# Four batches across the partitions in the gradient memory of a decoder block

## The reference, cut to what matters

```
k, v, q = causal_dwconv(hidden @ W.T)        # 32 features each, four taps
alpha, eta, theta = mean over 32 features of sigmoid / sigmoid / softplus gates
for c0 in range(0, S, CHUNK):                # 4 chunks, each needs the state of the one before
    g = grad of sum((silu(k_t @ W1.T) @ W2.T - v_t)**2), state of the chunk's start
    g = g * min(1 / norm(g), 1)              # per token
    Sm = eta*Sm - theta*g;  Wm = (1-alpha)*Wm + Sm      # a scan over the 64 tokens
    h = silu(q_t @ W1t);  out_t = h @ W2t    # with the state of each token
out = rmsnorm(retrieved @ Wo.T) * (hidden @ gW.T + gb); x = layernorm(x + out)
```

## Time and profile before

| | us |
|---|---|
| median of 3 runs (lowest, highest) | 4791.35 (4788.69, 4794.55) |
| profiled execution, its own time | 4782.92 |
| its span, first to last instruction | 4780.8 |
| `memory_inputs`, first matmul to the next block's first | 12.68 to 86.04 |
| the four `memory_chunk` blocks, to the last copy's end | 86.04 to 218.72 |
| `memory_output`, to its last copy's end | 219.69 to 256.74 |

### The profile page before, as it was taken

One profiled execution on the slowest core, in us unless ns is written; L12 is line 12 of the kernel. 1 busy time (PEld: TensorE's weight loads), 2 busy tenths in 40 slices (PEclk: granted clock), 3 DMA queues, 4 the chain that ended last, 5 costly groups with the idle time before them and its releaser, 6 DMA issues. The chain is left out here.

```text
span 4780.8 us, 75879 instructions
## 1 busy us (share of the span) xinstructions
PE 3821.7 (80%) x28979; PEld 2194.7 (46%) x28979; DVE 3405.9 (71%) x5269; ACT 2397.6 (50%) x3237; POOL 1424.3 (30%) x1078
## 2 busy tenths in 40 slices
PE   5740887999999999999983748849985858888873
PEld 3630445666666666666652424424433422222222
DVE  5478665778777877878784247667755658888868
ACT  2120224666666666666661125526662437776772
POOL 0000432666666666666673340000000000000000
PEclk6565898999999999999996769969996869999996
DMA  0010840000000000000002163145521342332300
GB/s 20 1 55 0 182 129 28 1 15 15 1 15 1 15 1 15 1 15 1 1 1 89 54 165 50 24 81 83 84 36 34 83 83 46 51 47 49 51 2 9
DMA packets 155463, 194.79 MB, mean 41 GB/s; under 512 B 23685, under 2 KB 117502, under 8 KB 154468
## 3 DMA queue, kind: packets, MB, share of 16 engines
q1 hardware_dynamic: 144068, 167.17, 17.5%
q0 software_dynamic: 9856, 22.67, 1.8%
q10 hardware_dynamic: 1184, 0.12, 0.0%
HBM read 145.03 MB, written 42.42 MB: 39 GB/s over the span
## 5 line engine op out<-in xcount | busy, mean ns | idle before, releaser
L3127 POOL TENSOR_TENSOR arena<-arena 128x512 f32<-128x512 f32 (+1 forms) x768 | 1133.0, 1477 | 630.1 <-ACT arena L3081 575.9
L2574 ACT ACTIVATE arena<-ps 128x1024 f32<-128x1024 f32 (+1 forms) x688 | 703.1, 1023 | 329.4 <-PE ps L2499 319.0
L2592 DVE TENSOR_REDUCE arena<-ps 128x2 f32<-128x826 f32 (+1 forms) x576 | 564.9, 981 | 183.4 <-PE ps L2445 175.1
L3143 DVE TENSOR_TENSOR arena<-arena 128x1024 f32<-128x1024 f32 (+1 forms) x448 | 653.1, 1497 | 34.9 <-ACT arena L3110 34.9
L3165 DVE TENSOR_TENSOR arena<-ps,arena 128x512 f32<-128x512 f32 (+1 forms) x768 | 530.3, 691 | 109.1 <-ACT arena L3075 75.6
L2445 PE MATMUL ps<-arena 48*128 48x413 bf16 (+3 forms) x1920 | 436.5, 334 | 132.2 <-DVE arena L2592 64.3
L3075 ACT ACTIVATE arena<-ps 128x1024 f32<-128x1024 f32 (+1 forms) x448 | 410.4, 960 | 200.6 <-PE ps L3003 194.2
L3081 ACT ACTIVATE arena<-arena 128x1024 f32<-128x1024 f32 (+1 forms) x448 | 425.0, 992 | 60.4 <-DVE arena L3143 57.9
L2518 PE MATMUL ps<-arena 128*9 128x256 f32 (+2 forms) x5504 | 436.1, 389 | 10.2 <-ACT arena L2562 7.4
L3003 PE MATMUL ps<-arena 64*128 64x256 f32 (+1 forms) x3328 | 427.4, 391 | 5.8 <-ACT arena L3097 1.3
L3017 PE MATMUL ps<-arena 128*64 128x256 f32 (+1 forms) x3328 | 411.1, 387 | 6.5 <-ACT arena L3081 6.5
(11 more groups left out here) (661 smaller groups left out, 5341.3 us busy)
## 6 DMA issues: line engine op xcount, KB each, us to landing
arena<-ctx_parts SPq DMA_DIRECT2D x96, 200.1 KB
arena<-ctx_parts SPq DMA_DIRECT2D x192, 100.1 KB
arena<-fs_rows SPq DMA_DIRECT2D x128, 128.0 KB, 7.2
arena<-in_ctx_feat SPq DMA_DIRECT2D x8, 1601.0 KB, 6.4
arena<-in_ctx SPq DMA_DIRECT2D x16, 768.0 KB
arena<-diff_att_stack SPq DMA_DIRECT2D x60, 192.0 KB, 6.6
ctx_parts<-arena SPq DMA_DIRECT2D x24, 400.2 KB, 7.7
arena<-in_ctx_feat SPq DMA_DIRECT2D x8, 800.5 KB, 9.4
```

Source lines behind the costliest of these rows:

```text
L2574: act.activation(self.prob[0:rows, u % 3, :], self.ps[0:rows, 2 * (u % 2):2 * (u % 2) + 2, :].rearrange("p n c -> p (n c)"), ACT.Exp).then ...
L2592: ins = dve.tensor_reduce(dst[:, :, j // 2], self.ps[:, 4:6, 0:hi - lo], AX.X, ALU.max)
L3127: pool.tensor_tensor(acc[0:rows, u % 2, :], before, sc[0:rows, u % 2, t, :], ALU.add).then_inc(added, 1)
L3143: dve.tensor_tensor(e, e, mb[0:rows, u % 2, None, :].to_broadcast([rows, n, 2 * S]), ALU.subtract).then_inc(sub_done, 1)
```

## The change

The eight batches become four groups q of two batches j. The four groups go across the partitions (32 features each, 128 in all) and the two batches stay in the columns. Column counts per instruction fall to a quarter: 512 in `memory_inputs`, 128 in a chunk. The states become block-diagonal 128x128 matrices (`state`, `W2`, `kM`, `h0M`, `GM`, `GM2`, `woM`, with zeros that POOL writes once), so that one matmul serves four batches. Where a product must stay 32 wide (projections, the clipped products `inside`, the updates), four matmuls write four different 32-partition groups of PSUM.

```diff
+            def project(bank, name, g):
+                for q in range(NQ):
+                    ins = pe.matmul(ps[rows_of(q), bank, :], W(name)[:, g * HM:(g + 1) * HM],
+                                    x_feat[:, q * BANK:(q + 1) * BANK], start=True, stop=True)
+                ins.then_inc(s["proj_ready"], 1)
...
-                ins = pe.matmul(ps[0:96, 4 + n, :], W("wgate"), x_feat[:, n * BANK:(n + 1) * BANK],
+            project(BANK_OF_GATE[ALPHA], "wgate", ALPHA)
+            project(BANK_OF_GATE[ETA], "wgate", ETA)
+            project(BANK_OF_PROJ[KEY], "wkvq", KEY)
+            project(BANK_OF_GATE[THETA], "wgate", THETA)
+            project(BANK_OF_PROJ[QUERY], "wkvq", QUERY)
+            project(BANK_OF_PROJ[VALUE], "wkvq", VALUE)
+
+            for n, g in enumerate((ALPHA, ETA)):
+                pe.wait_ge(s["sig_ready"], n + 1)
+                pe.matmul(ps[:, 6 + n, :], W("same"), gates[:, g, :], start=True,
+                          stop=True).then_inc(s["rates_f"], 1)
...
+            by_token(0, ALPHA)
...
+            by_token(2, ETA)
```

```diff
...
+            for c in range(NCH + 1):
+                if c:
+                    e = c - 1
+                    if e:
+                        pe.wait_ge(s["out_copied"], e)
+                    open_bank()
+                    carried(e, 0, feat["qA"][:, :, e, :], feat["qB"][:, :, e, :])
+                    pe.wait_ge(s["gm_ready"], c)
+                    pe.wait_ge(s["cg_ready"], c)
+                    inside(e, 1, GM).then_inc(s["y_ready"], 1)
+                if c < NCH:
+                    if c:
+                        pe.wait_ge(s["w1_ready"], c)
+                    for j in range(NJ):
+                        ins = pe.matmul(two(z)[:, j, :], state[:, c % 2, 0, 0, j, :], key[:, j, c, :], start=True, stop=True)
+                    ins.then_inc(s["z_ready"], 1)
+                    for q in range(NQ):
+                        ins = pe.matmul(ps[:, KQ, q * P:(q + 1) * P], kM[:, q, c * P:(c + 1) * P], query[:, :, c, :],
+                                        start=True, stop=True)
+                    ins.then_inc(s["kq_ready"], 1)
...
+                    for j in range(NJ):
+                        ins = pe.matmul(two(pred)[:, j, :], state[:, c % 2, 0, 1, j, :], two(h0[c % 2])[:, j, :],
+                                        start=True, stop=True)
+                    ins.then_inc(s["pred_ready"], 1)
+                    pe.transpose(turned_h, h0[c % 2], ident[:, :]).then_inc(s["turned_h"], 1)
+                if c:
+                    pe.wait_ge(s["h_ready"], c)
+                    pe.wait_ge(s["h0M_ready"], c)
+                    for q in range(NQ):
+                        ins = pe.matmul(ps[:, HH, q * P:(q + 1) * P], h0M[:, e % 2, q, :], h, start=True, stop=True)
+                    ins.then_inc(s["hh_ready"], 1)
...
+                    for j in range(NJ):
+                        ins = pe.matmul(two(pred)[:, j, :], W2[:, j, :], two(dp)[:, j, :], start=True, stop=True)
+                    ins.then_inc(s["dh_ready"], 1)
+                    pe.transpose(turned[:, 0:P], dp, ident[:, :])
...
+                if c:
+                    pe.wait_ge(s["hab_ready"], c)
+                    open_bank()
+                    carried(e, 1, two(hA), two(hB))
...
+                if c:
+                    pe.wait_ge(s["gm2_ready"], c)
+                    inside(e, 0, GM2).then_inc(s["out_ready"], 1)
+                if c < NCH - 1:
+                    pe.wait_ge(s["cgw1_ready"], c + 1)
+                    for j in range(NJ):
+                        for q in range(NQ):
+                            ins = pe.matmul(two(got[0])[rows_of(q), j, :], ktok[:, c, j, rows_of(q)], cgw[1][:, q, :, :],
+                                            start=True, stop=True)
+                    ins.then_inc(s["upd0_ready"], 1)
...
```

```diff
+                if 0 < c < NCH:
+                    dve.wait_ge(s["upd0_ready"], c)
+                    ins, src0 = renew(c, 0)
+                    ins.then_inc(s["w1_ready"], 1)
...
+                    link(ins)
+                    dve.transpose(W2[:, :, :], state[:, c % 2, 0, 1, :, :]).then_inc(s["w2_ready"], 1)
...
+                    dve.wait_ge(s["dh_ready"], c + 1)
+                    link(tt(da, pred, silu, ALU.mult))
+                    dve.sem_inc(s["da_ready"], 1)
...
+                    dve.wait_ge(s["norm_a_ready"], c + 1)
+                    at = slice(c * NQ, (c + 1) * NQ)
+                    link(tt(n2, norm_a, m["knorm"][:, at], ALU.mult))
+                    tt(n2, n2, np_h, ALU.add).then_inc(s["norm_ready"], 1)
+                    dve.wait_ge(s["root_ready"], c + 1)
...
+                        link(tt(coef_w[:, :, :], m["ends"][:, c, :, :], coef[:, :, None].to_broadcast([P, NQ, 2]), ALU.mult))
+                        for n, ready in ((1, "cgw1_ready"), (0, "cgw0_ready")):
+                            src = by_q(turned[:, n * P:(n + 1) * P])[:, :, None, :].to_broadcast([P, NQ, 2, HM])
+                            tt(cgw[n][:, :, :, :], src, coef_w[:, :, :, None].to_broadcast([P, NQ, 2, HM]),
+                               ALU.mult).then_inc(s[ready], 1)
```

```diff
-                ins = pe.matmul(out[:, t, :], m["ret"][:, t * P:(t + 1) * P], W("woT"), start=True, stop=True)
+            for n in range(4):
+                ins = pe.matmul(ps[:, n, :], m["ret"][:, n * P:(n + 1) * P], m["woM"][:, :, :], start=True, stop=True)
```

More of the change, by code:

```diff
@@ L391, in memory_inputs @@
         st = Stage(env, ctx, "mem_in")
[L392 to L399, removed]
@@ L422, in _ @@
[L422 to L431, removed]
@@ L440, in _ @@
+            pe.wait_ge(s["theta_in"], 1)
+            for c in range(NCH):
+                ins = pe.matmul(ps[:, 6, c * NQ:(c + 1) * NQ], theta[:, c * P:(c + 1) * P], means[:, :, 0],
+                                start=True, stop=True)
+            ins.then_inc(s["sums_ready"], 1)
         @block.scalar
         def _(act):
-            link = Chain(act, act_own)
-            act.wait_ge(gate_in, 1)
-            act.activation(gates[0:64, :], ps[0:64, 4:8, :], ACT.Sigmoid, bias=W("gate_b")[0:64, :]).then_inc(sig_ready, 1)
@@ new lines, in _ @@
+            act.wait_ge(s["kturn_ready"], 1)
+            for j in range(NJ):
+                copy(m["ktok"][half(j), :, j, :], ps[half(j), 7, :].rearrange("p (c f) -> p c f", f=P))
+        @block.gpsimd
+        def _(pool):
+            pool.memset(first[:, :, :], 0.0).then_inc(s["firsts_ready"], 1)
+            for name in ("state", "now", "W2", "kM", "ktok", "woM"):
+                ins = pool.memset(m[name], 0.0)
+            ins.then_inc(s["zeros_ready"], 1)
+            for name in ("h0M", "GM", "GM2", "htok", "zero"):
+                pool.memset(m[name], 0.0)
+            pool.wait_ge(s["soft_ready"], 1)
+            pool.tensor_tensor(chunk_first(theta), by_chunk(gates[:, THETA, :]), by_chunk(soft[0]),
+                               ALU.add).then_inc(s["theta_in"], 1)
@@ L466, in _ @@
[L466 to L482, removed]
@@ new lines, in open_bank, with carried, inside @@
+            def open_bank():
+                pe.matmul(yo, m["zero"][:, 0:P], m["zero"][:, P:2 * P], start=True, stop=False)
+            def carried(c, n, a, b):
+                for j in range(NJ):
+                    pe.matmul(two(yo)[:, j, :], state[:, c % 2, 0, n, j, :], a[:, j, :], start=False, stop=False)
+                    pe.matmul(two(yo)[:, j, :], state[:, c % 2, 1, n, j, :], b[:, j, :], start=False, stop=False)
+            def inside(c, n, g):
+                for q in range(NQ):
+                    ins = pe.matmul(yo[rows_of(q), :], cg[c % 2][:, n, q, :], g[:, q, :], start=False, stop=True)
+                return ins
```

537 lines of the change are left out of this document (298 added, 239 removed).

## The result

The changed kernel takes 4652.63 us (median of 4 runs, 4646.32 to 4663.57), the kernel before 4790.02 in the same rounds (4780.89 to 4794.55). The ratio is 0.9726, with an interval of 0.9706 to 0.9746: faster. Forecast: 4670, 121.4 us less. Measured: 137.4 less, then 119.8.

The account below looks back on a forecast made before the run. DVE was taken to set memory_inputs' end, one PE-ACT-DVE chain the chunks. Gains 42.7 (memory_inputs) + 78.0 (chunks) + 3.5 (memory_output) - 2.8 (array shapes) = 121.4, from 4782.92 to 4661.5, as median 4670; range 4651 to 4698.

Parts of the forecast that it names:

- Projections: In memory_inputs: 12 fourfold passes, 5.8 us, plus 1.5 for a start at half clock, 7.3 in all.
- DVE's list in `memory_inputs`: From the rates on, DVE sets the end of memory_inputs: its steps together 20.4 us.
- Weight slab: 27% larger, it lands under the turning of x before 12.68; without that cover it would cost 1.9 us.
- Rounds: Chunks: a round takes 16.0 us at half clock, 11.2 at full; clock rises and falls, so the middle, 13.6.
- Rival (2): Chunks: clock rises in the second round and stays, chunks 48 us, memory_output 2 less; total 4661; chance 0.15.
- Array shapes (0.1 each): Changes between column groups and full width cost 0.1 us, about seven a round, 2.8 over the program.
- The table loads that I counted as hidden: Chunks: both ACT table loads lie between other steps and cost nothing; uncovered, each would cost 1.3 us a round.
- (1): Clock stays at half in chunks and projections: rounds 16.0, last 21.9, projections and sums 4.8 more; 4683; chance 0.20.
- (3): 32-wide matmuls of projections, clipped groups and updates do not overlap: 34 us more, 4704; chance 0.06.
- (4): Slower than before: each of 240 32-wide passes waits for the one before to end, costing 108 us; chance 0.02.
- (5): Gain is there, but rounds carry unseen waits of 4 us each: 4686; chance 0.07.
- It would be wrong if stages behind change their pace: Sign of failure: everything behind memory_output's first DVE step, whose code is unchanged, was to stay the same.

Follow-up runs that it names:

- again: The changed kernel once more, nothing edited; single run 4650.40 us, with 110.19 up to memory_output's first DVE step and 4538.1 behind.
- qmajor: Changed kernel with the 24 projections ordered one column group after another instead of going round the four; 4648.61 us.
- dveoff: Changed kernel with four DVE steps of memory_inputs moved, two to ACT and two to POOL; 4645.14 us.
- warmfill: Changed kernel plus 26 unread matmuls ending memory_inputs and up to seven more each round where TensorE waits; single run 4665.95 us, timed again 4653.89.
- warm: Changed kernel plus 26 unread full-width matmuls in TensorE's idle time at the end of memory_inputs, rounds unchanged; single run 4646.42 us.
- nowarm: Changed kernel without the two small activations a round that only load the next ACT table; single run 4653.14 us.
- serial: Changed kernel with each chunk's output half after its own head, before the next head starts, not beside it; 4653.32 us.
- pause: Changed kernel plus 17 DVE memsets of 128x2048 ahead of memory_output's first DVE step; 4673.08 us.
- both: Changed kernel with the edits of dveoff and warmfill together, 11 fillers at the end of memory_inputs instead of 17; 4648.40 us, ratio to before 0.9743.

## Why the prediction held, and where its sizes were off

The forecast put `memory_output`'s first DVE step at 232.45 - 121.4 = 111.0; it came at 108.58. So the working is right within 2.5 us where it speaks, and the 13.5 us between the 137.4 of the first medians and these 123.9 lie behind it and did not repeat: the second set of runs gave 119.8. The first median is some 17 us under the forecast of 4670: 2.5 from the working, 9.7 from the part behind, and 5.0 because a median was taken to lie 8.4 over its profile and lay 3.5 over it. The low end of the range had been put there for overlap on DVE, which did not come; that 4652.63 still lies inside it is in part luck.

| step | forecast | measured |
|---|---|---|
| start of the projections | 12.68 | 12.26 |
| projections and sums, to the rates | 9.2 | 7.3 (9.1 in `again`) |
| DVE to the end of `memory_inputs` | 20.4 | 20.6 |
| chunks, with 2.8 for array shapes | 57.5 | 56.5 |
| `memory_output`, first matmul to first DVE step | 9.3 | 9.4 |
| two block changes | 1.94 | 2.54 |

- **Projections (7.3 forecast)**: 5.36 in the first profile, 7.11 and 7.19 in the other two. The 1.5 us more at the start, taken from L410, are there in some executions (the 0.86 between the first groups, twice 0.43) and not in others. That half clock is their cause is not shown: the record of the kernel before reads 1.00 over L410's passes too, and so the 0.96 of the earlier trace rows does not show that the projections raised the clock. The fourfold overlap held, and qmajor shows that it comes from going round the groups.
- **DVE's list in `memory_inputs`**: right to 0.2 us, and dveoff shows that nothing else stands within 3.4 us behind it.
- **Weight slab**: it is 29% larger (1202 columns against 935), not 27, and landed in 6.9 us where the smaller one took 7.0, so the 1.9 us that it would have cost without cover are not there.
- **Rounds**: 13.9 and 13.8 against 13.6 plus 0.7 for shapes. But this middle was taken between two ends, and the one that was measured was off: at full clock a round takes 12.1, not 11.2. DVE's work is 10.4 to 10.5 of it, 0.7 less than priced, and 1.6 us of gaps between its steps were missed; the longest in warmfill's third round are 0.38 behind the masked product on PE, in which the fillers may have a part, and 0.27 behind the root on ACT. The other end, 16.0, is not tested, since no round with an output half beside a head ran at 0.50 throughout. A line through 0.62 and 13.89 and through 1.00 and 12.14 gives 14.4 there, one through 0.62 and warm's 0.75 and 12.78 gives 14.9: estimates. The last window, with round 4, took 19.89 where 18.2 was forecast before shapes, and round 0 8.95 where 9.3 was; the sum came out by such errors against one another too. Rival (2) would have won 6.4 to 7.5 in the chunks, as the two profiles with fillers show; against it stand the 0.62 to 0.68 of the changed kernel itself and warm, where the clock was up and did not stay.
- **Array shapes (0.1 each)**: the passes of L637, two by four column groups of 128 columns, start at 79.87 and the next full-width matmul at 80.45. Two passes take 2 x 0.22 by the earlier trace rows, so the change took 0.14 here, at half clock, and seven a round about 1.0, an estimate from this one place. The Trainium skill says, in "TensorEngine Tiling (Array Packing)", Key Properties, that such a change drains TensorE. The 0.14 fits that; the row does not show that a drain is its cause.
- **The table loads that I counted as hidden**: right for what was built, but my price of 1.3 a round for each holds only for the root and only in rounds 1 to 3: 3.8 over the whole program for both (nowarm).
- **Rivals**: (1) fell with the mean clock of 0.62 to 0.68, though round 0 lay at 0.50 in the first profile. (3) and (4) fell with the 5.36 us; had the order been that of qmajor, 11.5 us would be gone. (5) fell with the rounds.
- **"It would be wrong if stages behind change their pace"**: they did, by up to 14 us within one kernel. This, not the change, is the distance between 121 and 137, and it lies mostly in the kernel before: its medians were 4790.02, 4771.32 (beside serial, qmajor and dveoff) and 4776.18 on three occasions, the changed kernel's 4652.63 and 4656.40.

Open: what sets the later part. Over 14 profiles it runs from 4528 (qmajor) to 4561 (warmfill), in the same code, and in the rows above the longer stage goes with the lower clock. Most of it is that one long stage, which begins some 3.7 ms into the program: it takes from 763.3 (qmajor, at 0.95) to 796.5 (warmfill_timed, at 0.92), the rest of the later part from 3759 to 3770. Three kernels with a longer part ahead (serial, qmajor, pause) have the shortest later part, 4528 to 4530, and the two profiles of warmfill the longest. The kernel before, 4548 and 4534, does not fit in, and neither does both, which has nearly the same fillers as warmfill: 4541.7 behind, the long stage 777.5 at 0.94. Whether work ahead costs clock behind, or both are chance, these runs don't tell.

## What to carry to other kernels

Where narrow matmuls wait for one another, turn the batch into column groups and go round the groups in the inner loop: four then cost one (5.36 against 15.70 us for the same 48 passes). A chain through several engines gains most from fewer, fuller steps, and less from work put beside it: 63 of the 76 us here (the four blocks made into one program among them), against 13. When a change touches 5% of a kernel, profile the unedited kernels twice before explaining the last 10 us, and read an edit of a few microseconds at its place, since the total may not show it.

## What the runs showed of the hardware that was not expected

- At the program's start the granted clock on record does not tell the pace: L433's window reads 1.00 both where its first groups of four stand 0.86 apart (`again`) and where all stand 0.43 apart (the first profile). What halves the pace there stays open.
- Passes of one column group follow one another at 0.43 us; in qmajor the whole came to 15.70 rather than 48 x 0.43 = 20.6, so groups also overlap at the place where the order turns from one to the next.
- Within the chunks' program a table load starts as soon as the activation before it is over, ahead of the wait for its own operand (47.49, the operand written from 49.90 on, in nowarm).
- TensorE's clock fell from 0.98 to 0.75 between one round and the next in warm, with PE busy 10.66 of 12.78 us, and stayed at 1.00 in warmfill with 11.36 of 12.15.
